# Attention stage with top-2 routing in it: power split, routing steps reordered, copies moved to ScalarE, last routing interleaved

## The reference

```python
h = _rmsnorm(x, ln1_w)
q = (h @ wq.T) ...; k = (h @ wk.T) ...; v = (h @ wv.T) ...      # 4 heads, 2 key/value heads
q = q * cos + _rotate_half(q) * sin                             # k alike
scores = jnp.where(causal, q @ k^T / sqrt(HD), -1e30)
y = softmax(scores) @ v
x = x + y @ wo.T
flat = _rmsnorm(x, ln2_w)
probs = softmax(flat @ router_w.T)
tp, ti = top_k(probs, 2)
...
```

## Time and profile before

| | us |
|---|---|
| median of three runs | 3415.86 (3410.84 to 3417.27) |
| the profiled execution | 3411.13 |
| its span, first to last instruction | 3409.4 |
| attention stage in it, 2575 to 3047.3 | 472.3 |
| DVE busy in that stage | 311.0 |
| PE, ACT and POOL busy in it | 303.2, 241.8, 158.3 |

### The profile page before, as it was taken

How to read it: one execution, slowest core, us unless ns; L and a number is a source line. 1 busy time by engine, 2 the same in 40 slices (tenths; PEclk the granted TensorE clock), 3 DMA queues, 4 the chain that set the end, 5 groups by cost and what they waited for, 6 DMA issues and landing times. The chain is left out here.

```text
span 3409.4 us, 68862 instructions
## 1 busy us (share of the span) xinstructions
PE 2626.2 (77%) x19386; PEld 2090.6 (61%) x19386; DVE 2287.1 (67%) x6715; ACT 1767.5 (52%) x5080; POOL 854.4 (25%) x844
## 2 busy tenths in 40 slices
PE   3999965991875923689999997898885777739993
PEld 2777755991775923566777765565562544429993
DVE  5777753566674665577777775688884777725555
ACT  1334323663663634556555553666663666516664
POOL 0233343661352523200000000000001234433442
PEclk9999987995886966899999998899997999959996
DMA  5112202234321213100000000000001000012225
GB/s 184 50 56 65 65 20 65 83 86 147 101 63 46 68 57 131 47 1 1 0 0 0 0 0 11 25 19 18 25 13 57 14 20 25 24 34 60 63 62 170
DMA packets 142548, 168.55 MB, mean 49 GB/s; under 512 B 19920, under 2 KB 118224, under 8 KB 141776
## 3 DMA queue, kind: packets, MB, share of 16 engines
q1 hardware_dynamic: 117744, 120.77, 11.7%
q0 software_dynamic: 21504, 44.74, 3.7%
q10 hardware_dynamic: 3168, 1.49, 0.2%
HBM read 115.87 MB, written 51.05 MB: 49 GB/s over the span
## 5 line engine op out<-in xcount | busy, mean ns | idle before, releaser
L1145 POOL DMA_INDIRECT y_rows<-ffn_e_rows_out,ffn_e_scatter_at x352 | 340.9, 969 | 435.3 <-DVE ffn_e_rows_out L1173 251.5
L1286 PE MATMUL bank<-ffn_e_xT,ffn_e_mine 128*128 128x128 f32 x3360 | 438.1, 277 | 2.1 <-ACT ffn_e_xT L1219 1.4
L1286 PEld LDWEIGHTS bank<-ffn_e_xT,ffn_e_mine 128*128 128x128 f32 x3360 | 408.8, 194 | 3.4 <-ACT ffn_e_xT L1219 2.2
L889 POOL DMA_INDIRECT sorted_rows<-ffn_r_h,ffn_r_slot x320 | 322.0, 1006 | 314.9 <-issue 314.6
L1221 ACT ACTIVATE ffn_e_mine<-constants 128x512 f32 (+1 forms) x352 | 250.1, 712 | 125.2 <-issue 77.3
L1193 DVE TENSOR_TENSOR ffn_e_hid<-ffn_e_act,bank 128x256 f32<-128x256 f32 (+1 forms) x280 | 136.0, 486 | 224.3 <-ACT ffn_e_act L1246 186.6
L1296 PE MATMUL bank<-ffn_e_mine,ffn_e_hid 128*128 128x128 f32 x1968 | 278.1, 276 | 2.3 <-DVE ffn_e_hid L1197 1.9
L1296 PEld LDWEIGHTS bank<-ffn_e_mine,ffn_e_hid 128*128 128x128 f32 x1968 | 247.5, 192 | 5.0 <-DVE ffn_e_hid L1197 4.5
L2487 ACT ACTIVATE gnn_prob<-bank,gnn_low 128x256 f32<-128x256 f32 x512 | 193.9, 490 | 51.9 <-DVE gnn_low L2405 51.9
L2405 DVE TENSOR_REDUCE gnn_low<-bank 128x2 f32<-128x512 f32 x256 | 158.9, 683 | 63.4 <-PE bank L2581 63.3
L2593 PE MATMUL bank<-ident,gnn_prob 128*128 128x128 f32 x1024 | 145.9, 277 | 42.7 <-DVE gnn_probT L2416 32.2
(11 more groups left out here) (504 smaller groups left out, 6617.8 us busy)
## 6 DMA issues: line engine op xcount, KB each, us to landing
g_adj<-in_adjT SPq DMA_DIRECT2D x48, 512.0 KB, 3.9
ffn_e_rows_in<-sorted_rows SPq DMA_DIRECT2D x346, 66.0 KB
ffn_c_y<-y_rows SPq DMA_DIRECT2D x80, 256.0 KB, 3.3
g_adj_rows<-in_adj SPq DMA_DIRECT2D x16, 512.0 KB, 4.2
gnn_adj<-in_adjT SPq DMA_DIRECT2D x16, 512.0 KB, 3.9
constants<-in_ffn SPq DMA_DIRECT2D x1, 6281.0 KB, 18.3
y_rows<-ffn_e_rows_out,ffn_e_scatter_at POOLq DMA_INDIRECT x352, 2.2
constants<-in_ffn SPq DMA_DIRECT2D x1, 5204.0 KB, 16.1
```

The costliest lines, as they stand in the source:

```text
L889: g.indirect_dma_start(self.c.sorted_rows, bass.IndirectOffsetOnAxis(self.slot[par][:, k, j:j + 1], 0), self.h[par][:, j, :], None).then_i ...
L1145: g.indirect_dma_start(c.y_rows, bass.IndirectOffsetOnAxis(scatter_at[par][:, k:k + 1], 0), rows_out[par][:, k, :], None).then_inc(scatter ...
L1286: ins = pe.matmul(chunk(part, ch), chunk(weights[:, i * HALF:(i + 1) * HALF], ch), x, start=True, stop=True)
```

## The change

1. The power of `mean_sq` is split: columns 0 to 7 (turns 0 and 1) first, columns 8 to 63 behind it, each with its factors; DVE starts `mean_sq` ahead of two casts, and GpSimd's `pool_begin` comes behind both powers. `rows_h(2)` waits for the second part.
2. In DVE's turn, `vector_first` moves from the end of turn t to behind `T(0, 0)` of turn t+1, and `vector_shift` from ahead of `rope_q` to behind `rope_q`, `T(0, 3)` and `vector_second`. On ScalarE, `scalar_rows` moves behind the second `evac_o`.
3. `ACT_T` grows from two copies in eight to four: heads 1 and 2 of both quads.
4. After the last turn, the routing of turns 13, 14 and 15 is interleaved with the end of attention and with each other, on all four engines. GpSimd's dispatches keep their order.

```diff
-    ACT_T = ((0, 2), (1, 2))
+    ACT_T = ((0, 1), (0, 2), (1, 1), (1, 2))
+    EARLY = 2 * TT
...
+                for at in (slice(0, EARLY), slice(EARLY, TILES)):
+                    if at.start == 0:
+                        g.wait_ge(square_ready, 1)
+                    g.tensor_tensor(rs2[:, at], mean_sq[:, at], c.minus_half[:, at], ALU.pow).then_inc(rs2_ready, 1)
                 route.pool_begin(g)
-                g.wait_ge(square_ready, 1)
-                g.tensor_tensor(rs2[:], mean_sq[:], c.minus_half[:], ALU.pow).then_inc(rs2_ready, 1)
...
+                factors(0, slice(0, EARLY))
                 v.tensor_copy(far16[:], w["far"])
                 v.tensor_copy(ident16[:], c.ident[:]).then_inc(once, 1)
...
                 rope_q(0, 0)
                 rope_k(0, 0)
+                factors(1, slice(EARLY, TILES))
...
                     T(0, 0)
+                    if since(t, 3):
+                        route.vector_first(v, t - 3, 1 - par, three)
                     if since(t, 2):
                         route.vector_stats(v, t - 2, two)
                     scores_low(t, 0)
-                    T(0, 1)
-                    if since(t, 2):
-                        route.vector_shift(v, t - 2, par, two)
                     if not last:
                         rope_q(t + 1, 1 - par)
                     T(0, 3)
                     if since(t, 3):
                         route.vector_second(v, t - 3, three)
+                    if since(t, 2):
+                        route.vector_shift(v, t - 2, par, two)
                     if not last:
                         rope_k(t + 1, 1 - par)
                     T(1, 0)
...
                     scores_low(t, 1)
-                    T(1, 1)
...
                         new_rows(t - 1)
-                    if since(t, 2):
-                        route.vector_first(v, t - 2, par, two)
                 every_turn(v, turn, begin=3)
...
+                A, B, Z = TURNS - 3, TURNS - 2, TURNS - 1
+                evac_T(Z, 1, 1, 0)
+                route.vector_first(v, A, A % 2, A + 1)
+                route.vector_second(v, A, A + 1)
+                route.vector_stats(v, B, B + 1)
+                evac_T(Z, 1, 1, 3)
+                route.vector_chosen(v, A, A + 1)
+                route.vector_shift(v, B, B % 2, B + 1)
+                norm_o(Z, 1)
+                route.vector_places(v, A, A % 2, A + 1)
+                route.vector_gates(v, A, A + 1)
+                new_rows(Z)
+                route.vector_stats(v, Z, Z + 1)
+                route.vector_first(v, B, B % 2, B + 1)
+                route.vector_second(v, B, B + 1)
+                route.vector_shift(v, Z, Z % 2, Z + 1)
+                route.vector_chosen(v, B, B + 1)
+                route.vector_places(v, B, B % 2, B + 1)
...
+                    T(0, 1)
                     exp(t, par, 0, 0)
                     exp(t, par, 0, 1)
+                    T(0, 2)
                     exp(t, par, 0, 2)
-                    T(0, 2)
                     exp(t, par, 0, 3)
                     if not first:
                         evac_o(t - 1, 0)
-                    if since(t, 2):
-                        route.scalar_rows(a, t - 2, par)
...
                         evac_o(t - 1, 1)
+                    if since(t, 2):
+                        route.scalar_rows(a, t - 2, par)
                     if not last:
                         evac_v(t + 1, 1 - par)
+                    T(1, 1)
                     exp(t, par, 1, 0)
...
-                pe.wait_ge(once, 1)
+                pe.wait_ge(once, 3)
...
+                outputs_T(Z, True)
+                route.tensor_rank(pe, A)
+                tokens_T(Z, True)
+                route.tensor_hT(pe, B, B % 2)
+                final(Z)
+                pe.wait_ge(route.picked, B)
+                route.tensor_logits(pe, B)
```

More of the change, by code:

```diff
@@ L2848, in turn @@
                         new_rows(t - 1)
-                    if since(t, 2):
-                        route.vector_first(v, t - 2, par, two)
                 every_turn(v, turn, begin=3)
-                for j in range(4):
-                    evac_T(TURNS - 1, 1, 1, j)
-                norm_o(TURNS - 1, 1)
-                new_rows(TURNS - 1)
-                route.vector_second(v, TURNS - 3, TURNS - 2)
-                route.vector_chosen(v, TURNS - 3, TURNS - 2)
-                route.vector_places(v, TURNS - 3, 1, TURNS - 2)
-                route.vector_gates(v, TURNS - 3, TURNS - 2)
-                for t in (TURNS - 2, TURNS - 1):
-                    route.vector_stats(v, t, t + 1)
-                    route.vector_shift(v, t, t % 2, t + 1)
-                    route.vector_first(v, t, t % 2, t + 1)
-                    route.vector_second(v, t, t + 1)
-                    route.vector_chosen(v, t, t + 1)
-                    route.vector_places(v, t, t % 2, t + 1)
-                    route.vector_gates(v, t, t + 1)
+                A, B, Z = TURNS - 3, TURNS - 2, TURNS - 1
[16 more added lines that the diff above has]
+                route.vector_places(v, B, B % 2, B + 1)
+                route.vector_gates(v, B, B + 1)
+                route.vector_first(v, Z, Z % 2, Z + 1)
+                route.vector_second(v, Z, Z + 1)
+                route.vector_chosen(v, Z, Z + 1)
+                route.vector_places(v, Z, Z % 2, Z + 1)
+                route.vector_gates(v, Z, Z + 1)
             @block.scalar
@@ L2872, in rows_h @@
                     wait_past(a, hT_ps, t)
+                    if isinstance(t, int) and t == EARLY // TT:
+                        a.wait_ge(rows_scaled, 2)
                     for k in range(TT):
@@ L2960, in _ @@
                 every_turn(a, turn, begin=3)
-                evac_T(TURNS - 1, 1, 1, 2)
-                evac_o(TURNS - 1, 0)
-                evac_o(TURNS - 1, 1)
-                evac_onT(TURNS - 1)
-                route.scalar_exp(a, TURNS - 3)
-                for t in (TURNS - 2, TURNS - 1):
-                    route.scalar_rows(a, t, t % 2)
-                    route.scalar_hT(a, t)
-                    route.scalar_exp(a, t)
+                A, B, Z = TURNS - 3, TURNS - 2, TURNS - 1
+                evac_T(Z, 1, 1, 1)
+                evac_T(Z, 1, 1, 2)
+                route.scalar_exp(a, A)
+                evac_o(Z, 0)
+                evac_o(Z, 1)
+                route.scalar_rows(a, B, B % 2)
+                evac_onT(Z)
+                route.scalar_hT(a, B)
+                route.scalar_exp(a, B)
+                route.scalar_rows(a, Z, Z % 2)
+                route.scalar_hT(a, Z)
+                route.scalar_exp(a, Z)
             @block.tensor
```

46 lines of the change are left out of this document (22 added, 24 removed).

## The result

| | us |
|---|---|
| after, undisturbed runs | 3364.07, 3367.04, 3378.81 |
| before, beside them, median of four | 3414.88 (3410.84 to 3417.27) |
| ratio | 0.9873, interval 0.9858 to 0.9887 |
| profiled execution after, and its span | 3364.07, 3362.3 |

A fourth execution of the changed kernel took 11.9 ms and is left out; with it in, the median of the four is 3372.93. The change makes the kernel 1.3% faster. In the two profiled executions the spans differ by 47.1 us, where the prediction's sum was 49.1. The three runs differ in TensorE's mean granted clock over the whole kernel: 0.907 and 0.906 in the two faster ones, 0.902 in the one of 3378.81.

A forecast was written before the change was run, and what follows sets the result against it. No engine was full; a ring of waits through GpSimd's dispatch set the turn. Start 9.4, turns 27.1 and end 12.6 sum to 49.1 us off 3411.13, giving 3362 profiled, 3366.8 for the median; stated 3364, range 3346 to 3388.

The forecast's parts named there:

- the mechanism of the turns: Turns 4 to 14: without the wait for the dispatch a turn falls from 23.63 to 21.36 us, 25.0 in all.
- Of the 4.2 us of the lower clock I count half, 2.1: Turns 4 to 14: 2.1 us come back because TensorE's idle stretch before k's projection is gone.
- the denser turn keeps the clock: Turns 4 to 14, by the skill's rule: TensorE's clock stays up, all 4.2 us come back, the sum would be 51.
- Moved copies and the first's new place there are worth 1 us either way: Turns 0 to 3 and 15: moved copies and `vector_first`'s new place change 1 us either way; counted as nothing.
- the start: Stage's beginning to `rope_q(0)`: 9.4 us less from the split power and earlier `mean_sq`, with the weights still in time.
- the end: Behind the last turns: interleaved routing of turns 13 to 15 ends the last dispatch earlier, 12.6 us less.
- The issue time of 9.9: End of the stage: GpSimd takes 9.9 us to issue a dispatch, read from turn 13's.
- The half microsecond counted for `new_rows` beside a dispatch: End of the stage: one `new_rows` beside a dispatch slows a DMA from 0.96 to 1.47 us, 0.5 off the gain.
- The 2 us that the prediction worked out for the small routing instructions: End of the stage, by the skill's port rule: small routing instructions beside a dispatch might cost some 2 us.
- ScalarE bounds the turn: Rival for the turns, chance 0.20: moved copies wait ahead of the exponents, turn 22.2, gain 40 us, 3374.
- The turn gets shorter: Rival for the turns, chance 0.13: better overlap gives a turn of 20.6, 8 us more gain; with full clock 3354.
- TensorE's clock: Rival for the turns, chance 0.05: at 1.2 GHz TensorE sets the turn, up to 30 us; all 11 turns give 3460.

The follow-up runs named there:

- Experiment 2: Kernel before the change with only `vector_shift` and `scalar_rows` moved to their new places: 3384.76 us, ratio 0.9917.
- experiment 1: Changed kernel with `vector_shift` and `scalar_rows` back in their old places: 3392.12 us, ratio 0.9945 to the kernel before.
- Experiment 5: Changed kernel with the first quad's product with v carried out twice, same result, 16 more matmuls a turn: 3356.28 us, ratio 0.9839.
- experiment 6: Changed kernel with `vector_first` back at the end of the turn: 3363.92 us, ratio 0.9861 to the kernel before.
- experiment 7: Changed kernel with the router's statistics, shift, second choice and ScalarE's exp of the gates later in the turn: 3348.41 us, ratio 0.9815.
- experiment 11: Kernel before the change with only the first quad's product carried out twice: 3414.62 us, ratio 1.0.
- Experiment 3: Changed kernel with the two added copies, `T(0,1)` and `T(1,1)`, back on DVE: 3363.99 us, ratio 0.9863 to the kernel before.
- Experiment 8: Changed kernel with the first piece of the power 16 columns wide in place of 8: 3371.43 us, ratio 0.9883.
- the second timing: The changed kernel itself, unaltered, timed again beside the second group of experiments: 3368.59 us, ratio 0.9878 to the kernel before.
- experiment 9: Kernel of experiment 7 with the first quad's product also carried out twice: 3350.03 us, ratio 0.9816.
- experiment 10: Kernel of experiment 9 with the router's gates moved behind DVE's last copy: 3352.19 us, ratio 0.982.

## Why the prediction was right, and where it was off

**Right: the mechanism of the turns.** The dispatch's wait is gone, a plain turn is 21.28 where 21.36 was laid out, and the steps within it agree to 0.2 us. Experiment 2 shows that the move of the shift does all of this by itself; experiment 1 that without it the turns gain nothing. Rows of one turn, added by hand in the new order, were enough for the plain turn.

**Off by 5.7 us: the term "Of the 4.2 us of the lower clock I count half, 2.1".** The excess went from 4.2 to 7.8, not to 2.1; the plain turns, 21.28 for 21.36, gave 0.9 of it back, so the turns are 4.9 short. The reason given, that the idle stretch before k's projection is gone, named the right place, but 1.6 us of idle time remain ahead of the last transposes before it and 0.68 ahead of it (rows 2840.02 and 2841.21 below), and the clock falls in just this place. The step to "the denser turn keeps the clock" failed: PE is busy 81% of the stretch, not 73%, and the clock falls five times as before. The term also took the cost of a fall for its number: before, two of the five fell where DVE didn't wait and cost nothing; now all five fall on k's projection.

```profile
2840.02 0.52 PE L3050 MATMUL bank<-ident,att_prob 128*128 128x128 f32 x3 [1.61 <-ACT att_probT L2924]
2841.21 1.45 PE L3018 MATMUL bank<-att_hT,constants 128*128 128x512 f32 x2 [0.68 <-DVE att_qT L2779]
```

Experiment 5 shows that with 16 matmuls more just ahead of there the clock falls once, and experiments 6 and 7 that with other orders it falls twice or once. The Trainium skill, "TensorE: Matmul & The Clock Gate", Part 1, has the throttled clock as the default and activity as what releases it; experiment 5 agrees (242 to 235 us in the turns), experiment 11 doesn't (264 to 265, and six falls for five).

**Off by 1 us or more: "Moved copies and the first's new place there are worth 1 us either way".** For turns 0 to 3 it left out what the start does to the clock: 2.7 of the 3.3 us. For the loop the prediction gave the first's new place no price of its own; by experiments 2, 3 and 6 it is 4 to 6 us lost, almost all of it in turns with a fall of the clock.

**Right: the start**, 9.7 for 9.4, with the weights hidden. Experiment 8 gives the slope once more: the power of 16 columns takes 2.91, 1.25 more than the 1.66 of 8 columns.

**Off by 1.4: the end**, 11.2 for 12.6. The dispatch of turn 15 comes 12.03 behind that of turn 14, where 10.2 was laid out; the stop behind the first DMA is 1.85 over the usual 0.30. The issue time of 9.9 was read from turn 13's row, which has no stop. The half microsecond counted for `new_rows` beside a dispatch was 0.15, because the DMA began later beside the add. The Trainium skill, "SBUF — State Buffer", "Who interferes with whom", has VectorE and GpSimd hold one port pair in turns; the trace agrees for the add of 0.69 us, 0.15 here. The 2 us that the prediction worked out for the small routing instructions are not in the trace: beside them the DMAs follow each other at 1.26 us as in the undisturbed dispatches.

**The rivals.** *ScalarE bounds the turn*: no. Experiment 3 takes the two copies off it and changes nothing. *The turn gets shorter*: not here, but experiment 7 reaches 20.24 with another order, below the 20.6 of that rival. *TensorE's clock*: the mechanism was the right one to fear, and its size 7.8 us, 3.6 more than before, not tens.

**The stated time.** The sum gave 3362 for the profiled execution, which took 3364. For a typical run it gave 3366.8, and I wrote 3364; the second timing is 3368.6.

**Open.** What exactly makes TensorE's clock fall in some turns, and why its falls moved onto k's projection. Experiments 5 and 11 contradict any rule in which more matmuls are enough; which of position, distance and length of the gaps decides was not separated. Open too are the stop of 2.15 us, the start of experiments 8 to 10, and the 1.2 us lost and 2.0 won outside the stage in unchanged code, which other pairs of executions show in other sizes.

## What to carry to other kernels

A wait for a DMA that recurs in every turn is taken away by moving the waiting instruction behind work that needs nothing from it; that one move was worth 27 us, and the rest of the change together 17. When a turn is then set by one engine's order, count what stands between its two slowest releases: 1.1 us taken out of there gave 1.04. Price TensorE's clock per turn, from the rows of the turns at either level, and look at what TensorE is doing when it falls: a fall under a matmul for which nobody waits cost nothing, the same fall under one on the path 1.3 to 1.7 us. Two orders with nearly the same plain turn differ by 6 us in this way. The quickest kernel here, that of experiment 7, has both, a turn shorter by 1.04 and one fall in place of five.

## What was new about the hardware

- TensorE's clock fell five times in the same eleven turns before and after the change. On q's projection, for which DVE did not wait before the change, a fall cost nothing (turns of 23.65 and 23.61 for 23.63); on k's it cost 1.3 to 1.7 us.
- Sixteen extra matmuls in a turn took 6.5 us off the eleven turns and 12.3 off the kernel: the clock fell once, not five times. The same extra work in the kernel before changed nothing (ratio 1.0, six falls for five).
- After 14.3 us without work TensorE starts at 0.50 and is at the higher level some 6 us after its first matmul in eight profiles; in two others, after the same 14.3 us, it takes more than 23. After 23.9 us without work it takes more than 16, in three profiles.
- The power on GpSimd costs 1.66 us for 8 columns, 2.91 for 16, 9.29 for 56 and 10.58 for 64: 0.16 us a column and some 0.4 besides.
- An indirect DMA's issue beside a VectorE add of two SBUF operands takes longer by about what is left of the add: 0.51 with 0.64 left, 0.15 with 0.27 left. An issue that began first was not slowed.
- In a row of eight indirect DMAs one issue stops, always behind the first DMA of the dispatch of turn 14: for 1.65 us in four profiles of kernels with the old end, for 2.15 in ten with the new one.
